# Second attention of a two-layer gated network: scores transposed, fp32 value products, running sums of exponentials on GpSimd

## The reference

```
x = x + tanh(g_xattn[1]) * attention(layernorm(x), ctx, ctx)

attention(q, k, v):            # 4 batches, 8 heads of 64 rows, 512 x 512
    # the second axis (position) is split into the heads' channels
    attn = einsum('bct,bcs->bts', qh * scale, kh * scale)      # scale = 1/8
    attn = softmax(attn, axis=-1)
    out  = einsum('bts,bcs->bct', attn, vh)
```

## Time and profile before

| | |
|---|---|
| median of three runs | 1676.54 us (1673.2 to 1680.06) |
| profiled execution, its own time | 1677.74 us |
| its span in the trace | 1676.0 us |
| mean granted TensorE clock | 0.901 of full speed |
| attention stage: first transfer issued | 751.93 us |
| attention stage: first scores | 783.2 us |
| last stage begins | 1060.1 us |
| first gate product of the last stage | 1073.1 us |
| busy over the span: PE, DVE, ACT, POOL | 80%, 74%, 46%, 19% |

### The profile page before, as it was taken

One profiled execution on the slowest core, in us unless ns is written; L12 is line 12 of the kernel. 1 busy time (PEld: TensorE's weight loads), 2 busy tenths in 40 slices (PEclk: granted clock), 3 DMA queues, 4 the chain that ended last, 5 costly groups with the idle time before them and its releaser, 6 DMA issues. The chain is left out here.

```text
span 1676.0 us, 24635 instructions
## 1 busy us (share of the span) xinstructions
PE 1346.0 (80%) x8976; PEld 758.8 (45%) x9000; DVE 1241.5 (74%) x1952; ACT 767.8 (46%) x1451; POOL 325.5 (19%) x233
## 2 busy tenths in 40 slices
PE   5599993636868989873967759679999999999996
PEld 3378773212334444432645546334444444444443
DVE  5567777825558778956999999488877777887764
ACT  3445562715334444424978879323333334433322
POOL 0032424607445557531000000000000000000000
PEclk8789996558888999996979889789999999999998
DMA  8312231355142242226030000000000000000000
GB/s 290 117 52 61 102 101 41 128 147 157 55 131 83 90 124 88 101 67 247 3 125 0 25 0 0 1 1 7 6 6 13 6 6 6 6 6 9 10 6 13
DMA packets 56493, 102.17 MB, mean 61 GB/s; under 512 B 9823, under 2 KB 20727, under 8 KB 56300
## 3 DMA queue, kind: packets, MB, share of 16 engines
q1 hardware_dynamic: 55148, 97.14, 17.5%
q0 software_dynamic: 1280, 4.20, 0.9%
HBM read 73.47 MB, written 27.66 MB: 60 GB/s over the span
## 5 line engine op out<-in xcount | busy, mean ns | idle before, releaser
L2084 PE MATMUL HG<-W1H,XT 128*128 128x512 f16 x512 | 166.6, 387 | 27.2 <-ACT XT L2045 20.7
L1558 PE MATMUL FD<-W0D,HH 128*128 128x512 f16 x512 | 159.6, 395 | 14.8 <-DMA W0D<-down_weights,IDX 12.2
L2084 PE MATMUL HU<-W1H,XT 128*128 128x512 f16 x512 | 163.2, 380 | 0.0
L2110 PE MATMUL HD<-W1H,HT 128*128 128x512 f16 x512 | 155.2, 380 | 0.0
L1552 PE MATMUL FG<-F,W0G 97*128 97x512 f16 x324 | 86.1, 400 | 52.9 <-DMA F<-features_kept 24.5
L2053 ACT ACTIVATE SG<-HG,DS 128x512 f32<-128x512 f32 x64 | 43.9, 686 | 160.6 <-PE HU L2084 160.6
L1805 ACT ACTIVATE PR<-A_S,NM,CM 128x512 f32<-128x512 f32 x128 | 99.5, 777 | 34.2 <-DVE NM L1946 34.2
L2187 DVE SCALAR_TENSOR_TENSOR H<-HU,DS,SG 128x512 f32<-128x512 f32 x64 | 48.0, 750 | 87.6 <-ACT SG L2053 85.7
L1442 POOL TENSOR_TENSOR HL<-HM,HH 128x512 f16<-128x512 f32 x64 | 92.3, 1442 | 86.0 <-ACT HH L1481 85.5
L335 ACT ACTIVATE DD<-E,TM 128x128 f32<-128x128 f32 x256 | 72.7, 369 | 70.3 <-PE E L431 68.7
L1558 PE MATMUL FD<-W0D,HL 128*128 128x512 f16 x256 | 100.1, 391 | 0.0
(11 more groups left out here) (335 smaller groups left out, 3369.8 us busy)
## 6 DMA issues: line engine op xcount, KB each, us to landing
VALP<-in_ffn_weights_dram SPq DMA_DIRECT2D x24, 512.0 KB, 3.6
VALQ<-in_ffn_weights_dram SPq DMA_DIRECT2D x24, 512.0 KB, 3.6
quantised_weights<-QQ SPq DMA_DIRECT2D x24, 512.0 KB, 2.8
X<-in_x_dram SPq DMA_DIRECT2D x8, 1024.0 KB, 6.0
CTX<-in_ctx_dram SPq DMA_DIRECT2D x8, 1024.0 KB, 5.6
W1H<-quantised_weights SPq DMA_DIRECT2D x3, 2048.0 KB, 10.6
W1L<-quantised_weights SPq DMA_DIRECT2D x3, 2048.0 KB, 15.4
F<-features_kept SPq DMA_DIRECT2D x16, 288.0 KB
```

The source lines that it names most:

```text
L1558: last = pe.matmul(DN[c][:, :], lhs[:, i, c * P:(c + 1) * P], W2[:, i, part, :], start=(i == 0 and n == 0), stop=(i == KI - 1 and n == 2))
L2084: ins = pe.matmul(bank[:, :], lhs, rhs, start=(i == 0), stop=(i == len(terms) - 1))
L2110: ins = pe.matmul(DN[0][:, :], HT[:, q, lp, k, :], W[:, 2, i * D:(i + 1) * D], start=(i == 0 and lp == 0 and W is WH), stop=(i == KI - 1 a ...
```

## The change

The scores are made transposed: keys on the partitions, queries along the row, so that the exponentials are already what the value product needs and no transposes are wanted. Two heads, one in the upper and one in the lower 64 rows, are taken together, without padding. A step is one pair of heads and 128 keys: 64 steps in all, in 8 quads of 8 steps (two pairs). The maximum over the keys, now across partitions, is got from separate products in the old orientation (`largest`, high halves only), one per step, for the quad ahead; VectorE reduces them (`slot`), makes a bfloat16 high and low part, TensorE turns these into rows, and a rank-two product with ones adds the negative maximum to the scores. The exponentials stay fp32 and go straight into fp32 value products, 64 columns of the array per head. Their sums over keys are formed by GpSimd additions and one fp32 product with ones per pair; VectorE takes the reciprocal of 128 x 512, SyncE copies rows of it to the right partitions with eight transfers per quad, VectorE multiplies the outputs, GpSimd adds them to X. The context, XN, values and both halves of keys and queries are laid in the room of the up and down weights; keys and queries, values and maxima rows are double-buffered, so the next batch is prepared during the steps. The low up weights and the down weights are loaded at the start of the last stage.

The diff, cut to its core (removed lines are those of `attention_phase` above; new lines only):

```diff
+SLOTS = ((0, None), (1, 2), (3, None), (4, 5), (6, None), (7, None), (None, None), (None, None))
...
+    CTX, XN = (WH1[:, 1, i * 2 * NC * S:(i + 1) * 2 * NC * S].bitcast(F32).rearrange("p (c d) -> p c d", c=NC) for i in range(2))
+    VT = WH1[:, 2, :].bitcast(F32).rearrange("p (a j c) -> p a j c", a=2, j=NC)
+    K2 = WL1[:, 1, :].rearrange("p (a l c s) -> p a l c s", a=2, l=2, c=NC)
+    Q2 = WL1[:, 2, :].rearrange("p (a l c t) -> p a l c t", a=2, l=2, c=NC)
+    MX = stack.enter_context(nc.psum_tensor("A_M", [P, 2, S], F32))
...
+    def context(b):
+        if b:
+            sp.wait_ge(kl_ready, b)
+            sp.wait_ge(vt_turned, NC * b)
+        sp.dma_start(CTX[:, :, :], ctx[b]).then_inc(ctx_in[b], 16)
+    def spread(g):
+        sp.wait_ge(r_ready, g + 1)
+        for q in range(2):
+            if g:
+                sp.wait_ge(rep_taken, 2 * g + q - 1)
+            for par, r in enumerate(half):
+                row = 64 * q + 32 * par
+                for at in range(r.start, r.stop, 32):
+                    sp.dma_start(RB[at:at + 32, q, :], R4[row:row + 32, :]).then_inc(rep_in[q], 16)
...
+    for g in range(QUADS):
+        if g:
+            spread(g - 1)
+        if g % 2 == 1 and g // 2 + 2 < B:
+            context(g // 2 + 2)
+        if g == 5:
+            sp.wait_ge(kl_ready, B)
+            sp.wait_ge(vt_turned, NC * B)
+            sp.wait_ge(ql_ready, B)
+            weights(1, 0)
...
+    def residual(g):
+        for q in range(2):
+            c = 2 * g + q
+            pool.wait_ge(rep_taken, c + 1)
+            x = X[:, c, :]
+            pool.tensor_tensor(x, x, OS[:, c % OUTS, :], ALU.add).then_inc(x_added, 1)
...
+    for k in range(STEPS_A):
+        g, step = divmod(k, 8)
+        j, b = k % NC, g // 2 + 1
+        pool.wait_ge(p_ready, k + 1)
+        if step == 1 and g >= 2:
+            pool.wait_ge(all_ready, g - 1)
+        for par in range(2):
+            s = SS[:, g % 2, 2 * (step // NC) + par, :]
+            if j == 1:
+                ins = pool.tensor_tensor(s, PT[:, (k - 1) % RING, par, :], PT[:, k % RING, par, :], ALU.add)
+            elif j > 1:
+                pool.wait_ge(pool_own, n_own + par - 1)
+                ins = pool.tensor_tensor(s, s, PT[:, k % RING, par, :], ALU.add)
+            if j in (1, 2):
+                ins.then_inc(pool_own, 1)
+            elif j == 3:
+                ins.then_inc(sum_ready, 1)
+        if j in (1, 2):
+            n_own += 2
+        if j:
+            pool.wait_ge(pool_own if j < 3 else sum_ready, n_own if j < 3 else 2 * (k // NC + 1))
+            pool.sem_inc(added, 1)
+        if step == 2 and g % 2 == 0 and b < B:
+            scale(b)
+        if step == 4 and g >= 2:
+            residual(g - 2)
+        if step == 6 and g % 2 == 1 and b < B:
+            low(b)
+    for g in range(QUADS - 2, QUADS):
+        residual(g)
...
+    for k in range(STEPS_A):
+        g, step = divmod(k, 8)
+        b = g // 2 + 1
+        act.wait_ge(s_ready, k + 1)
+        if k >= RING:
+            act.wait_ge(o_ready, k - RING + 1)
+            done = k - RING if (k - RING) % NC else k - RING + 1
+            act.wait_ge(added, done - done // NC)
+        nc.scalar.activation(PT[:, k % RING, :, :], SB[k % 2][:, :, :], ACT.Exp,
+                             scale=CM[:, (g // 2) % 2, 5:6]).then_inc(p_ready, 1)
+        if k % NC == 0 and k:
+            unscaled(k // NC - 1)
+        if g % 2 == 0 and b < B:
+            if VT_STEP <= step < VT_STEP + NC:
+                values(b, step - VT_STEP, TB[:, :])
+            if step == 2:
+                deviation(b)
+            if step in (4, 5):
+                keys(b, slice(2 * (step - 4), 2 * (step - 4) + 2))
+            if step == 6:
+                queries(b)
+            if step == 7:
+                high(b)
+        if step == 7 and g + 1 < QUADS:
+            negated(g + 1)
...
+    def largest(g, i):
...
+        bank = first_bank(g, i)
+        for par, r in enumerate(half):
+            last = pe.matmul(bank[:, par, :], Q2[r, b % 2, 0, c, q * P:(q + 1) * P], K2[r, b % 2, 0, c, :],
+                             start=True, stop=True)
+        last.then_inc(mx_ready, 1)
...
+    def scores(k):
...
+        if k >= 2:
+            pe.wait_ge(p_ready, k - 1)
+        bank = SB[k % 2]
+        for i, (kp, qp) in enumerate(((0, 0), (1, 0), (0, 1))):
+            for par, r in enumerate(half):
+                pe.matmul(bank[:, par, :], K2[r, b % 2, kp, c, cols], Q2[r, b % 2, qp, c, :], start=(i == 0), stop=False)
+        for par in range(2):
+            row = 32 * (2 * (step // NC) + par)
+            last = pe.matmul(bank[:, par, :], ONES[row:row + 2, :], MB[row:row + 2, g % 2, :], start=False, stop=True)
+        last.then_inc(s_ready, 1)
+    def weigh(k):
+        b, pair, j = k // 16, k // NC, k % NC
+        c = pair % NC
+        pe.wait_ge(p_ready, k + 1)
+        if j == 0:
+            pe.wait_ge(vt_ready, NC * (b + 1))
+            if pair:
+                pe.wait_ge(o_taken, pair)
+        for par, r in enumerate(half):
+            last = pe.matmul(OB[r, :], VT[:, b % 2, j, c * P + par * AC:c * P + (par + 1) * AC],
+                             PT[:, k % RING, par, :], start=(j == 0), stop=(j == NC - 1))
+        last.then_inc(o_ready, 1)
+    def sums(g):
+        pe.wait_ge(sum_ready, 4 * (g + 1))
+        if g:
+            pe.wait_ge(r_ready, g)
+        for i in range(4):
+            last = pe.matmul(TB[32 * i:32 * i + 32, :], ONE[:, :], SS[:, g % 2, i, :], start=True, stop=True)
+        last.then_inc(all_ready, 1)
...
+    for k in range(STEPS_A):
+        g, step = divmod(k, 8)
+        b = g // 2 + 1
+        more = g + 1 < QUADS
+        before, behind = SLOTS[step]
+        if step == 7:
+            weigh(k)
+        if k + 1 < STEPS_A:
+            scores(k + 1)
+        if more and before is not None:
+            largest(g + 1, before)
+        if g % 2 == 0 and b < B and VT_STEP <= step < VT_STEP + NC:
+            j = step - VT_STEP
+            if j:
+                pe.wait_ge(vt_ready, NC * b + j)
+            elif g:
+                pe.wait_ge(r_ready, g - 1)
+            turn(b, j, TB)
+        if step < 7:
+            weigh(k)
+        if more and behind is not None:
+            largest(g + 1, behind)
+        if step == 6:
+            if more:
+                negatives(g + 1)
+            if g:
+                if g % 2 == 0 and b < B:
+                    pe.wait_ge(vt_ready, NC * (b + 1))
+                sums(g - 1)
+    sums(QUADS - 1)
...
+    def inverse_sums(g):
+        v.wait_ge(all_ready, g + 1)
+        if g:
+            for q in range(2):
+                v.wait_ge(rep_in[q], 64 * g)
+        v.reciprocal(R4[:, :], TB[:, :]).then_inc(r_ready, 1)
+    def normalise(g, q):
+        c = 2 * g + q
+        v.wait_ge(rep_in[q], 64 * (g + 1))
+        v.wait_ge(o_taken, c + 1)
+        o = OS[:, c % OUTS, :]
+        v.tensor_tensor(o, o, RB[:, q, :], ALU.mult).then_inc(rep_taken, 1)
...
+    for g in range(QUADS):
+        b = g // 2 + 1
+        even = g % 2 == 0 and b < B
+        odd = g % 2 == 1 and b < B
+        for i in range(8):
+            if g + 1 < QUADS:
+                slot(g + 1, i)
+            if even:
+                if i == 0:
+                    statistics(b)
+                elif i == 1:
+                    top(b)
+                elif i == 2:
+                    inverse(b)
+                elif i == 3:
+                    scale(b)
+            if odd and i == 4:
+                low(b)
+            if g >= 2 and i in (5, 6):
+                normalise(g - 2, i - 5)
+        if g + 1 < QUADS:
+            negatives(g + 1)
+        if g:
+            inverse_sums(g - 1)
+    for q in range(2):
+        normalise(QUADS - 2, q)
+    inverse_sums(QUADS - 1)
+    for q in range(2):
+        normalise(QUADS - 1, q)
...
+    for t, part, W, loaded in ((1, 1, WL, up_loaded), (2, 0, WH, down_loaded), (2, 1, WL, down_loaded)):
+        sp.dma_start(W[:, t, :].rearrange("p (q c) -> p q c", c=QT),
+                     store[t * QTILES:(t + 1) * QTILES, part].rearrange("q p c -> p q c")).then_inc(loaded, 16)
...
     def gate_up_products(tt, i):
+        pe.wait_ge(up_loaded, 16)
...
     def down_products(n):
+        pe.wait_ge(down_loaded, 32)
```

More of the change, by code:

```diff
@@ new lines, in _ @@
+            scale(0)
+            low(0)
+            n_own = 0
+            for k in range(STEPS_A):
[26 more added lines that the diff above has]
+                    low(b)
@@ new lines, in unscaled @@
+            def unscaled(pair):
+                act.wait_ge(o_ready, (pair + 1) * NC)
+                if pair >= OUTS:
+                    act.wait_ge(x_added, pair - OUTS + 1)
+                nc.scalar.copy(OS[:, pair % OUTS, :], OB[:, :]).then_inc(o_taken, 1)
+            act.wait_ge(consts, CONSTS + 1)
+            deviation(0)
+            queries(0)
+            high(0)
+            keys(0, slice(0, NC))
+            for j in range(NC):
```

(52 more changed lines are left out.)

364 lines of the change are left out of this document (143 added, 221 removed).

## The result

The changed kernel takes 1665.94 us (median of 8 runs, 1662.99 to 1670.67) against 1676.3 us (8 runs beside them): a ratio of 0.9939, 95% interval 0.9921 to 0.9958, 0.6% faster. Forecast were 1624.0 us. The range holds the result, the gain is a fifth of the one forecast. The profiled execution took 1662.99 us, its span is 1661.2 against 1676.0.

A forecast was written before the change was run, and what follows sets the result against it. VectorE was taken to pace the units, with bare turnovers between batches. Start, quads and end, 786.6 + 205.5 + 13.3 = 1005.4 against 1060.1, gave 1677.74 - 54.7 + 1 (weights) = 1624.0 us; range 1594 to 1690.

The forecast's parts named there:

- Prices: Operation times in the quads: exponential 1.15 us, reduction 1.21, reciprocal 3.4, GpSimd addition 1.28; TensorE step 2.40.
- not side by side: Rival: TensorE's paired matmuls run one after another, 1.94 us more a step, 124 in all: 1748 us; chance 0.05.
- the estimate with the Trainium skill's drain of roughly 175 ns: TensorE's four mode changes per step cost 0.70 us in place of 0.46, 15 us over 64 steps; not adopted.
- Start: Preparation before the quads: context at 757.5, GpSimd's first reduction before the scale at 769.9, ready for scores at 786.6 us.
- Contexts late: Contexts 2 and 3, queued behind eight small transfers, hold up VectorE's maxima: 5 us charged in each of quads 2 and 4.
- Waits among four engines as full as this cost something: Waits in the eight quads: factor 1.09 from the old kernel's fullest engine raises 188.5 us to 205.5.
- chains between engines: Rival: TensorE and VectorE alternate on one maxima buffer, about 3.6 us a step, 230 over 64: 1649 us; chance 0.20.
- the granted clock as now: Expected sign in the attention: TensorE's granted clock stays as before, 0.96 in the units.
- Even: 14 x 1.28 = 17.9, plus 0.4 ... no bound: GpSimd in even quads: additions, reduction and residual waits come to 20.3 us, so GpSimd doesn't bound the quads.
- the rival with 1.95: Rival: GpSimd's additions decide, slower than before from 1.95 us each; 1726 us at 2.33 each; chance 0.12.
- End: Bare chain behind the last step: additions, sums, reciprocal, transfers, last product and residual, 13.3 us.
- Weights behind the border: Three 2 MB weight transfers moved to the last stage's start: 1 us uncovered.

The follow-up runs named there:

- fills_only: Changed kernel, TensorE keeps all products of the maxima, but VectorE's reductions after the first quad and TensorE's wait for them are left out: 1642.51 us.
- act_late: Changed kernel with reordered preparation, shorter end, later batches' context maximum through memory by ScalarE's transfers, scale after the negatives, keys later: 1626.96 us, 0.9708 of the kernel before.
- order3_dma: Changed kernel with context load, statistics and low queries earlier; batches 1 to 3's maximum across partitions through memory by SyncE, not GpSimd: 1667.39 us.
- all_parts: order3_dma with a shorter end: two inverse buffers, last inverse before quad 6's normalisations, later residual, last four small transfers issued by ScalarE: 1665.86 us.

## Why the prediction was wrong

- **Prices: right.** Exponential 1113 ns (1.15), reduction 1221 (1.21), reciprocal 3357 (3.4), addition 1280 (1.28). In the last quad, at a granted clock of 1.00, a step takes 2.08 us; the forecast 2.40 less the maxima's pair and its change is 2.07. One step of TensorE, from value products to value products:

```profile
1012.83 1.08 PE L1986 MATMUL A_O<-PT,W1H 128*64 128x512 f32 x4
1013.84 0.82 PE L1971 MATMUL A_S<-W1L 64*128 64x512 f16 x6
1014.59 0.39 PE L1974 MATMUL A_S<-MB,ONES 2*128 2x512 bf16 x2
1014.91 1.08 PE L1986 MATMUL A_O<-PT,W1H 128*64 128x512 f32 x4
```

Six float16 records take 0.75 us to the start of what follows, where one after another at 0.216 they would need 1.30: "not side by side" falls. So does the estimate with the Trainium skill's drain of roughly 175 ns ("TensorE: Matmul & The Clock Gate", Single matmul latency) for each change: three of them in place of 0.12 each would make the step 2.25.
- **Start: 9.9 us too long.** First scores at 776.7, forecast 786.6. GpSimd's first reduction came at 759.42, not 769: its stand began at 751.5 and lay beside the context's load, before its input was there.
- **Contexts late: right** in kind. 5 us were charged in quads 2 and 4; TensorE stood 7.28 in quad 2.
- **The failed step: "Waits among four engines as full as this cost something; before, the fullest lost 59.80 / 54.91 = 1.09, which gives 205.5."** Measured are 248 / 188.5 = 1.32. The 1.09 came from a kernel that one engine paced. Here TensorE and VectorE hand one buffer of maxima back and forth 56 times in the quads, and whatever else stands in either list is paid by both. fills_only against the change shows 20.5 us for the reductions and these waits together. This is the rival "chains between engines", whose mechanism was right for half of the loss; that its 3.6 us per step is near the 248 / 64 = 3.9 measured is in part luck, for these also hold the context's part and the slower clock.
- **The clock, put at nothing:** "the granted clock as now" was 0.96 in a batch's units and is 0.86 over the quads. The eight quads have 173.2 us of TensorE's work in the forecast (3 x 23.7 + 4 x 20.9 + 18.5); it was busy for 196.0, though in the last quad, at 1.00, for 19.5 against 18.5. So a part of the loss, an estimated 15 us by these rows, is TensorE's work at its lower level. No run changes the clock alone.
- **A second failed step: "Even: 14 x 1.28 = 17.9, plus 0.4 ... no bound".** 0.4 was the reduction's own time. The 11.14 us of issue beside it in the earlier trace rows were used for the start and not for the even quads, where a stand comes before and behind: 13.9 us each. GpSimd is then at 33 us, over the 30.8 forecast for quads 2 and 4. Without the maxima it is their bound (33.0 and 36.1 us, 25.9 each without the reduction). In the changed kernel it is not: they take 40.5 and 41.7 us, and 40.6 and 42.7 with the reduction left out. It doesn't make the kernel slower than before, and additions cost 1.28, so the rival with 1.95 falls.
- **End: 13.3 forecast, 22.0 measured.** The last sums waited for GpSimd until 1029.2, 5 us behind the last value product and not 2.4; the reciprocal waited 2.8 more for two normalisations; eight small transfers take 5.0 us to issue, 0.62 each and not 0.30, so the second half lands late.
- **Weights behind the border:** 1 us forecast; 13.3 us to the first gate product after 13.0.

Start -9.9, quads +41.8 (247.3 us from the first scores on), end +8.7: the border comes 40.6 us later than the forecast 1005.4. Behind it 615.2 us follow where 616.9 were forecast, -1.7. That is 38.9 of the 39.0 us between 1624.0 and the profiled execution, which lies 3 below the median. The start's 9.9 us hide a fifth of the 50.5 lost in the quads and the end; that the parts partly cancel is luck.

## What to carry to other kernels

Price waits by where two engines share one buffer, not by a ratio from a kernel that one engine paced: list what else stands in both engines' lists between two hand-overs, and add it to both. A cause can hide behind another: taking GpSimd's reduction out made the attention no shorter by itself and 27 us shorter once the lists were in order and the maxima gone (14 with the maxima, part of it spread), so test a suspect again after the first bound is gone. And put a wait for something far away (a context, a trip through memory) behind the work that others wait for, not into its middle: the same trip through memory gave 1667 us in one place and, with its neighbours moved, 1627 in another.

## What the runs showed that was not expected

- GpSimd stands 5.9 to 6.7 us before a reduction across partitions that follows additions, and 6.7 to 7.5 us before the next addition (in the quads of all runs with the reduction). A reduction that follows a reduction has no such stand (0.1 us, kernel before), and a stand that falls into idle time costs nothing, like the first one of the preparation.
- After a long stand TensorE went on at its lower level. Without maxima it stood 11.02 us for the low queries; the granted clock was 0.50 (1.2 GHz) in the 7.5 us behind it, where six score records took 1.46 us and a value pair 1.98, and 1.00 (2.4 GHz) from 899.2 on, with 0.82 and 1.08:

```profile
866.00:878.00 12.00, 12.00 (x74) 3.09 (x72) 3.13 (x4) 6.91 (x8) 10.78 (x10) 1.00 0.00 0
890.00:897.50 7.50, 7.34 (x28) 1.50 (x28) 2.29 (x1) 2.70 (x3) 4.46 (x4) 0.50 0.19 72
899.20:903.00 3.80, 3.80 (x27) 1.28 (x26) 0.00 (x0) 2.04 (x3) 2.46 (x2) 1.00 0.00 0
```

So this stand was paid twice. Over the quads the granted clock is 0.86 in the change and 0.92 in act_late, where TensorE waits less.
- A small write and a read back through memory take 11.3 to 12.2 us from the first issue to landing when one engine issues them back to back (six times, order3_dma and all_parts), 6.6 to 7.5 of them before the second issue.
